# Attention scores spread by an accumulating transfer, with count columns and a filled-in shift, in a graph network kernel

## What is computed

```python
# layer 0: messages of edges, summed by node, then a dense update of every node
messages = mish(mish(cat(x[src], x[dst], edge_attr) @ W1 + b1) @ W2 + b2)
agg = segment_sum(messages, dst)
out = x + mish(cat(x, agg) @ W3 + b3) @ W4 + b4
# layer 1: mean over neighbours, then a normalisation over all nodes by column
agg = segment_sum(x[src], dst) / maximum(deg, 1)
out = agg @ W_l + b_l + x @ W_r
out = (out - mean(out, 0)) * rsqrt(var(out, 0) + EPS) * gamma + beta
out = where(out >= 0, out, 0.01 * out) + x
# layer 2: filters of an edge times rows of its nodes, summed by node (few columns)
# layer 3: attention over the edges, in 8 heads
aw = einsum(q[src], k[dst]); m = segment_max(aw, src)
e = exp(aw - m[src]); out = segment_sum(e / segment_sum(e, src)[src] * v[dst], src)
```

## Time and profile before

| | us |
|---|---|
| runs | 2187.74, 2193.56, 2196.75 |
| median | 2193.56 |
| profiled execution, its own time | 2185.32 |
| its span in the profile | 2183.6 |
| busy: PE, DVE, ACT, POOL | 1809.6, 1495.4, 1149.0, 939.1 |
| share of the span: PE, DVE, ACT, POOL | 83%, 68%, 53%, 43% |
| mean granted TensorE clock | 0.896 |

### The profile page before, as it was taken

The page is one execution under the profiler, slowest core; times in us unless marked ns, Lnnn a source line. Parts: engine busy times, 40 slices in busy tenths (PEclk is TensorE's granted clock), DMA queues, the critical chain, the costliest instruction groups (busy, mean ns, idle before and its releaser), DMA issues. The chain is left out here.

```text
span 2183.6 us, 24152 instructions
## 1 busy us (share of the span) xinstructions
PE 1809.6 (83%) x5525; PEld 939.7 (43%) x5525; DVE 1495.4 (68%) x2634; ACT 1149.0 (53%) x2356; POOL 939.1 (43%) x1051
## 2 busy tenths in 40 slices
PE   5999999599999999999999996932881698888830
PEld 2444444244444444444444443511771354444410
DVE  5365555167777777777777764927985788888857
ACT  1354434255555555555555542224884877777744
POOL 2211101156666666666666665644553022222126
PEclk9999999799999999999999998965555789999965
DMA  7652102534444444444444436664556555554444
GB/s 252 239 194 66 25 11 34 135 131 169 169 169 169 164 161 161 160 164 169 169 169 168 163 137 228 122 112 159 115 108 194 196 179 194 174 184 175 151 146 152
DMA packets 147582, 334.99 MB, mean 153 GB/s; under 512 B 18833, under 2 KB 19314, under 8 KB 146998
## 3 DMA queue, kind: packets, MB, share of 16 engines
q1 hardware_dynamic: 114726, 245.97, 32.4%
q0 software_dynamic: 29440, 83.69, 15.5%
q10 hardware_dynamic: 3344, 4.51, 0.6%
HBM read 181.92 MB, written 152.90 MB: 153 GB/s over the span
## 5 line engine op out<-in xcount | busy, mean ns | idle before, releaser
L668 PE MATMUL d_p_h<-w3a,d_xT 128*128 128x512 f32 x632 | 286.4, 596 | 23.1 <-DMA d_xT<-in_xT 23.1
L668 PE MATMUL d_p_o<-d_w,d_uT 128*128 128x512 f32 x632 | 286.9, 597 | 3.0 <-ACT d_uT L743 3.0
L668 PE MATMUL d_p_p<-d_wr,d_x1T 128*128 128x512 f32 x632 | 285.3, 594 | 0.0
L552 POOL TENSOR_SCALAR d_small<-d_mv 128x1 f32<-128x1 f32 x158 | 80.9, 512 | 301.3 <-DVE d_mv L794 153.3
L825 DVE TENSOR_TENSOR d_zz<-d_yg,d_xbeta 128x512 f32<-128x512 f32 x79 | 136.8, 1732 | 97.4 <-POOL d_yg L876 97.4
L668 PEld LDWEIGHTS d_p_h<-w3a,d_xT 128*128 128x128 f32 x632 | 120.9, 192 | 176.0 <-issue 176.0
L668 PEld LDWEIGHTS d_p_o<-d_w,d_uT 128*128 128x128 f32 x632 | 120.7, 192 | 155.4 <-issue 150.7
L736 ACT ACTIVATE d_yn<-d_y,d_small 128x512 f32<-128x512 f32 x79 | 64.3, 814 | 229.7 <-POOL d_small L557 229.7
L668 PEld LDWEIGHTS d_p_p<-d_wr,d_x1T 128*128 128x128 f32 x632 | 114.5, 191 | 114.5 <-issue 114.5
L764 ACT ACTIVATE d_x<-d_zz,d_small 128x512 f32<-128x512 f32 x79 | 64.3, 814 | 176.6 <-POOL d_small L557 176.6
L284 PE MATMUL m_p_H<-m_xT,m_w 128*128 128x512 f32 x320 | 147.5, 616 | 4.8 <-ACT m_xT L325 4.8
(11 more groups left out here) (285 smaller groups left out, 4231.0 us busy)
## 6 DMA issues: line engine op xcount, KB each, us to landing
state<-d_empty SPq DMA_DIRECT2D x80, 264.0 KB, 2.4
sum<-m_tile_sum SPq DMA_DIRECT2D x10, 2048.0 KB, 7.8
update<-d_empty SPq DMA_DIRECT2D x80, 256.0 KB, 2.3
pair_rows<-p_rows SPq DMA_DIRECT2D x40, 512.0 KB, 3.7
pair_x<-x SPq DMA_DIRECT2D x40, 512.0 KB, 4.6
out_rows<-pair_rows SPq DMA_DIRECT2D x40, 512.0 KB, 2.7
d_xT<-in_xT SPq DMA_DIRECT2D x79, 256.0 KB, 2.8
d_z<-sum SPq DMA_DIRECT2D x79, 256.0 KB, 3.0
```

Of the source, the lines that this page charges most:

```text
L552: nc.gpsimd.tensor_scalar(tmp, var, factor, add, ALU.mult, ALU.add).then_inc(done, 1)
L668: last = nc.tensor.matmul(out[:, :], lhsT[:, c, :], w[:, c, :], start=(c == 0), stop=(c == KB - 1))
```

## The change

The scores are stored as a row of 1024 numbers in DRAM (by a transfer that ACT issues), and one accumulating transfer by GpSimd (`spread_scores`) adds this row to all 128 partitions of `cand`, which ACT has laid out with 0 and `-BIG` (1024 columns now, where `away` had 128). The turn, the 8 matmuls, ACT's copy and DVE's addition go. In the steps of DVE, `pair_means` and `softplus` come ahead of `tile_maximum`; on ACT, `scores_out` comes directly behind `away_from`.

`sum0` gets 16 more columns, `COUNT`, filled with 0 and scatter-added with 1. The dense phase loads them by a transfer of its own for each tile, and DVE multiplies what it adds to the column sums with 1 where the count is 0, else with 0; so the aggregate phase has no old rows to gather and to subtract.

For all pairs but the first three (`PLAIN`) the shift is not added by DVE: at the end of the edge-rows phase DVE makes `quotient = shift / scale`; SP fills the buffer of the pair with it (`pair_fill`, in place of the load), and GpSimd adds `p` with an accumulating transfer (`pair_add_p`).

```diff
+COUNT = 16
...
+PLAIN = 3
...
+    k.sum0 = nc.dram_tensor("sum0_counted", [ROWS, D + COUNT], F32).ap()
...
-                             b3_row.rearrange("p (a d) -> p a d", a=1).to_broadcast([P, some, D])
+                             tile_sum[:, 0:1, :].to_broadcast([P, some, D + COUNT])
...
+                    pool.memset(tile_sum[:, :, D:D + COUNT], 1.0).then_inc(counts_set, 1)
+                    pool.wait_ge(counts_set, 2)
...
-                sp.dma_start(z[b][:, :], rows(k.sum0, i)).then_inc(z_in[b], 16)
+                sp.dma_start(z[b][:, :], rows(k.sum0, i)[:, 0:D]).then_inc(z_in[b], 16)
...
+            def load_count(i, b):
+                if not first(i):
+                    sp.wait_ge(alone_done, i - 1)
+                sp.dma_start(count[b][:, :], rows(k.sum0, i)[:, D:D + COUNT]).then_inc(count_in[b], 16)
...
+                dve.wait_ge(count_in[b], landed(i, b))
+                if not first(i):
+                    dve.wait_ge(acc_done, 2 * i - 2)
+                nc.vector.tensor_scalar(alone[b][:, :], count[b][:, 0:1], 0.0, None, ALU.is_equal).then_inc(alone_done, 1)
+                dve.wait_ge(alone_done, i + 1)
                 dve.wait_ge(row_done, i + 1)
...
-                        nc.vector.tensor_tensor(k.column_acc[0:valid, s, :], k.column_acc[0:valid, s, :],
-                                                part[b][0:valid, :], ALU.add).then_inc(acc_done, 1)
+                        nc.vector.scalar_tensor_tensor(
+                            out=k.column_acc[0:valid, s, :], in0=part[b][0:valid, :], scalar=alone[b][0:valid, 0:1],
+                            in1=k.column_acc[0:valid, s, :], op0=ALU.mult, op1=ALU.add).then_inc(acc_done, 1)
...
-            sp.wait_ge(corrected, 2 * T)
...
-            def gather_old(t):
-                pool.indirect_dma_start(old[:, t, :], None, k.p[:, :], at_rows(k.index[:, 1, t:t + 1])
-                                        ).then_inc(old_in, 16)
-
             pool.iota(dummy_i[:, :], [[0, 1]], base=N + P, channel_multiplier=1).then_inc(dummy_set, 1)
-            for t in range(3):
+            asked = 10
...
-            for t in range(T):
-                gather_old(t)
-                if t % 3 == 2:
-                    gather_x1(asked)
-                    asked += 1
-            pool.wait_ge(old_in, 16 * T)
...
-            dve.wait_ge(old_in, 16 * T)
-            for t in range(T):
-                if t >= 2:
-                    dve.wait_ge(corrected, 2 * t - 2)
-                nc.vector.tensor_tensor(square[t % 2][:, :], old[:, t, :], old[:, t, :], ALU.mult).then_inc(old_sq, 1)
-                correct(0, old[:, t, :], k.minus_share[:, t:t + 1])
-                dve.wait_ge(old_sq, t + 1)
-                correct(1, square[t % 2][:, :], k.minus_share[:, t:t + 1])
...
+def pair_fill(nc, k, sp, j):
+
+    b = j % ROW_BUFS
+    if j >= ROW_BUFS:
+        sp.wait_ge(k.pair_gone[b], 16 * (j // ROW_BUFS))
+    else:
+        sp.wait_ge(k.quotient_done, 1)
+    sp.dma_start(k.pair_rows[b][:, :, :], k.quotient[:, :].rearrange("p (a d) -> p a d", a=1).to_broadcast([P, 2, D])
+                 ).then_inc(k.pair_filled[b], 16)
+
+
+def pair_add_p(nc, k, pool, j):
+    b = j % ROW_BUFS
+    pool.wait_ge(k.pair_filled[b], 16 * filled_times(j))
+    nc.gpsimd.dma_start(k.pair_rows[b][:, :, :], rows_of_pair(k.p, j), accum_op=ALU.add).then_inc(k.pair_added[b], 16)
...
-    dve.wait_ge(k.pair_p_in[b], 16 * (j // ROW_BUFS + 1))
+    if j < PLAIN:
+        dve.wait_ge(k.pair_p_in[b], 16)
+    else:
+        dve.wait_ge(k.pair_added[b], 16 * filled_times(j))
     nc.vector.tensor_tensor(a, a, wide(k.bn_scale), ALU.mult).then_inc(k.pair_scaled, 1)
     dve.wait_ge(k.pair_scaled, j + 1)
-    nc.vector.tensor_tensor(a, a, wide(k.bn_shift), ALU.add).then_inc(k.pair_shifted, 1)
-    dve.wait_ge(k.pair_shifted, j + 1)
+    if j < PLAIN:
+        nc.vector.tensor_tensor(a, a, wide(k.bn_shift), ALU.add).then_inc(k.pair_shifted, 1)
+        dve.wait_ge(k.pair_shifted, j + 1)
     nc.vector.scalar_tensor_tensor(out=a, in0=a, scalar=0.01, in1=a, op0=ALU.mult, op1=ALU.max
...
+            scale, small, n = k.bn_scale[:, :], a[0][:, 0, :], 0
+            for f in (lambda: nc.vector.tensor_tensor(small, scale, scale, ALU.mult),
+                      lambda: nc.vector.tensor_scalar(small, small, 1e-36, 1e-18, ALU.is_lt, ALU.mult),
+                      lambda: nc.vector.tensor_tensor(scale, scale, small, ALU.add),
+                      lambda: nc.vector.reciprocal(small, scale)):
+                f().then_inc(k.quotient_steps, 1)
+                n += 1
+                dve.wait_ge(k.quotient_steps, n)
+            nc.vector.tensor_tensor(k.quotient[:, :], k.bn_shift[:, :], small, ALU.mult).then_inc(k.quotient_done, 1)
...
+            def spread_scores(t):
+                pool.wait_ge(aw_out, 16 * (t + 1))
+                pool.wait_ge(away_done, t + 1)
+                nc.gpsimd.dma_start(cand, k.score_rows[t:t + 1, :].to_broadcast([P, P * HEADS]), accum_op=ALU.add
+                                    ).then_inc(cand_in, 16)
...
+                if 0 <= t + 1 < T:
+                    spread_scores(t + 1)
                 if 0 <= t < T:
                     scatter_state(t)
                     if t + 1 < T:
                         gather_state(t + 1)
                 if step + 2 < T:
                     gather_rows(step + 2)
+                if step + 1 < STEPS:
+                    for j in range(given, given + HERE[step + 1]):
+                        pair_add_p(nc, k, pool, j)
+                    given += HERE[step + 1]
...
-            def turn_scores(t):
-                pe.wait_ge(aw_done, t + 1)
-                nc.tensor.transpose(p_k[0:HEADS, 0:P], k.scores[:, t, :], k.ident[:, :]).then_inc(aw_turned, 1)
-
-            def spread_scores(t):
-
-                pe.wait_ge(aw_out, t + 1)
-                if t:
-                    pe.wait_ge(part_done, t)
-                else:
-                    pe.wait_ge(heads_set, 2)
-                for h in range(HEADS):
-                    last = nc.tensor.matmul(p_S[:, h // 4, (h % 4) * P:(h % 4 + 1) * P], head_rows[0:HEADS, h, :],
-                                            scoresT[:, :], start=True, stop=True)
-                last.then_inc(spread_done, 1)
...
-                act.wait_ge(aw_turned, t + 1)
-                if t:
-                    act.wait_ge(spread_done, t)
-                nc.scalar.activation(scoresT[:, :], p_k[0:HEADS, 0:P], ACT.Copy).then_inc(aw_out, 1)
+                act.wait_ge(aw_done, t + 1)
+                act.dma_start(k.score_rows[t, :].rearrange("(p h) -> p h", h=HEADS), k.scores[:, t, :]
+                              ).then_inc(aw_out, 16)
 
             def away_from(t):
                 if t:
-                    act.wait_ge(cand_done, t)
+                    act.wait_ge(top_done, t)
                 same = k.same_src[:, t, :] if t < T - 1 else k.same_src_last[:, :]
-                nc.scalar.activation(away[:, :], same, ACT.Copy, bias=-BIG, scale=BIG).then_inc(away_done, 1)
+                nc.scalar.activation(cand.rearrange("p (e h) -> p e h", h=HEADS),
+                                     same.rearrange("p (e a) -> p e a", a=1).to_broadcast([P, P, HEADS]),
+                                     ACT.Copy, bias=-BIG, scale=BIG).then_inc(away_done, 1)
...
+                    scores_out(d)
                 if 0 <= c < T:
                     x3_turned_out(c, 0)
                     x3_turned_out(c, 1)
@@ -1847,8 +1877,6 @@
                     tile_normalise(nc, k, act, u)
                 if 0 <= c < T:
                     query_out(c)
-                if 0 <= d < T:
-                    scores_out(d)
...
-                dve.wait_ge(spread_done, t + 1)
-                dve.wait_ge(away_done, t + 1)
-                if t:
-                    dve.wait_ge(top_done, t)
-                nc.vector.tensor_tensor(cand[:, :, :], p_S[:, :, :].rearrange("p a (h e) -> p (a h) e", h=HEADS // 2),
-                                        away[:, :].rearrange("p (a e) -> p a e", a=1).to_broadcast([P, HEADS, P]),
-                                        ALU.add).then_inc(cand_done, 1)
-                dve.wait_ge(cand_done, t + 1)
+                dve.wait_ge(cand_in, 16 * (t + 1))
                 if t >= 2:
                     dve.wait_ge(fall_done, t - 1)
-                nc.vector.tensor_reduce(top, cand[:, :, :], AX_X, ALU.max).then_inc(top_done, 1)
+                nc.vector.tensor_reduce(top, cand.rearrange("p (e h) -> p h e", h=HEADS), AX_X, ALU.max).then_inc(top_done, 1)
...
+                    softplus(a)
                 if 0 <= d < T:
                     tile_maximum(d)
-                if HERE[step]:
-                    pair_means(nc, k, dve, pair)
-                if 0 <= d < T:
                     weigh_values(d)
-                if a < T:
-                    softplus(a)
                 for j in range(pair + 1, pair + HERE[step]):
```

(8 more changed lines are left out.)

77 lines of the change are left out of this document (40 added, 37 removed).

## The result

The changed kernel took 2230.78 us, the median of its runs (2228.61 to 2235.67), beside 2192.33 (2187.74 to 2196.75) for the kernel before. The ratio is 1.0179, with a 95% interval from 1.0150 to 1.0208. The profiled execution took 2228.76 us with a span of 2226.8, which is 43.2 over the 2183.6 before. The medians are only 38.5 apart: the profiled execution of the kernel before took 2185.32, less than any of its other runs.

What follows compares the result with a forecast made beforehand. The values phase was taken as bound by a loop of waits through ACT's list, no engine. 2185.3 - 10.5 + 5 + 12 + 34 = 2225.8, with 8.2 from profiled execution to median 2234 us; range 2184 to 2280.

Steps and rivals of the forecast that it cites:

- Aggregate phase: Twenty gathers and 60 DVE operations go, so the last pair of scatter-adds starts earlier: -10.5 us (-11 to -8).
- Message phase: Six serial scatter-adds at the end with wider rows, 0.8 us more each: +5 us (0 to +12).
- Dense and edge-rows phases: Added count work and the quotient's operations lie under cover: 0 (0 to +3) and 0 (0 to +2) us.
- Start of the values phase: Fill and accumulation behind each other make pairs later in the first four steps: +12 us (0 to +20).
- The steady step: Values phase: 18.85 us a step becomes 20.85, 2.0 more over 17 intervals: +34 us (+5 to +70).
- The clock's term: Values phase: PE idles before the queries, which run partly at half clock, +1.7 us a step (0 to 3.0).
- The floor of 19.15: Values phase step without loss of clock, by DVE's way to `less` and ACT's list: 0.3 us over 18.85.
- The row of scores: Values phase: store 2.2 us, GpSimd's issue and spread 7.0 land at S + 9.3 (S: issue of `scores_out`), 0.6 to spare.
- The full transfer engines (3): Rival, chance 0.13: the transfer engines become the bound in the values phase, a step of 23 us, median 2270.
- The gain (4): Rival, chance 0.15: DVE no longer late, ACT's list sets the values step at 17.1 us, median 2158.
- The rival without a loss of clock (2): Rival, chance 0.20: the same values loop at full clock, 0.3 us more a step, median 2205.
- that all is covered (5): Rival, chance 0.10: values step stays 18.85 us, start slips by 5, the aggregate's gain pays for it, median 2193.

Runs made afterwards that it cites:

- e6: The changed kernel with the spread of the scores taken back, count columns, fills and accumulating loads kept: 2164.28 us.
- e10: e4 with matmuls of 256 columns in TensorE's idle stretches, 4 ahead of the turns and 6 ahead of the queries each step: 2196.75 us.
- e4: The kernel before with the count columns alone, so no old rows in the aggregate phase: 2168.46 us.
- e5: The changed kernel with pairs loaded plain and the shift added by VectorE; spread and count columns kept: 2221.95 us.
- e1: The changed kernel with VectorE's tile_maximum put back ahead of pair_means and softplus: 2231.90 us.
- e3: The changed kernel with matmuls of 256 columns added, 4 ahead of the turns and 6 ahead of the queries each step: 2211.15 us.
- e7: e1 with the store of the scores issued by GpSimd as soon as they are there, not by ScalarE: 2244.84 us.
- e9: e5 with the maximum put first, the edit of e1: 2186.20 us.
- e13: e9 with the matmuls of e3 added, a wait for second_out ahead of them: 2175.93 us.
- e12: e6 with the first 10 pairs loaded plain, not 3: 2154.93 us, ratio 0.983 to the kernel before.
- e2: The changed kernel with cand laid out head by head for a contiguous maximum, the scores stored in 4-byte pieces: 2357.76 us.

## Why the prediction came out as it did

The forecast was 2234 with a range from 2184 to 2280; measured were 2230.78. The sign, the size and the likeliest case held. Not every step behind them did.

- **What bounded the kernel.** Right: the values phase is a loop of waits, no engine's busy time. The fills and accumulations of e6 lie beside the loop and cost nothing in the steady step; ten more matmuls a step do not (e10), so TensorE, 0.87 busy in e4, is close to the loop as well.
- **Aggregate phase.** Right: -11.0 for -10.5, since the last pair now waits for its tile (4.50, for `dst_rows_sb`) and no longer for the pair before it; e4 shows the same 11.3 by itself.
- **Message phase.** Mis-sized: +5 forecast, -1.3 measured, and the last start varies by 4.7 without a change. The serial scatter-adds went from 5.53 to 5.58 apart, where I had 0.8 more each (4.8 to land before, 4.9 now). A row's 64 additional bytes cost by their bytes, at most; the end of the bound that I moved away from was the right one.
- **Dense and edge-rows phases.** Right: +0.1 and +0.7, within what these phases vary by.
- **Start of the values phase.** Right in mechanism: VectorE waits 4.57, 3.93 and 5.68 for its first three accumulated pairs, where the earlier trace rows has 3.46 for a plain one. The fills cost 11.7 up to the fifth `away` beside the spread (e5) and 2.9 without it (e6 against e4), for 12 forecast; up to the first `away` the kernel after loses 4.7.
- **The steady step.** Right in direction, mis-sized, and near the table's row partly by luck. I had +2.0 on 18.85; steps of the same kind went from 18.95 to 21.76, +2.8. Over the first 17 intervals, as many as the sum had, the loss is 47.6 where I had 34. In the total this is made up by the message phase, which I had 6.3 too high, and by the start, if the 12 of the forecast are set beside the 4.7 up to the first `away`. The clock's term held: the queries took 75.0 us in 13 steps, 5.8 each, and 4.1 in the kernel before over 12 steps, so 1.6 for 1.7. But how long TensorE was idle directly ahead of them, from which I argued, does not tell it: they took 5.17 behind 3.00 and 6.53 behind 2.20.
- **The chain behind the step's floor.** The floor of 19.15 was worked out along the wrong chain. I let VectorE run from the merge through the residual without a stop, and put the queries on ScalarE's list only; in truth the residual waits for ScalarE's copy `f_y`, which stands behind the query's copy. So the dip of the clock reaches `less` through VectorE, and the 2.5 us of work that VectorE lost are idle time in its waits for `factor` and `f_y`. The maximum, which I took at 1.22, took 2.00: no row showed a stride of 8, and I had set no bound for it. These 0.8 are as much as lies between +2.0 and +2.8; that they are the cause is not shown, since no run takes the stride away by itself.
- **The row of scores.** I gave it 0.6 us of slack. Its place was right: e1 put the maximum 2.7 us earlier, and the row was late at once by 2.4. Its parts were not: the spread landed 5.3 after its issue, not 7.0, and the store took about 2.1 in one step and 4.7 to 6.5 in the next in most steps, beside the pairs' accumulations, where I had 2.2 for all. By the rule of the Trainium skill ("DMA: Bandwidth & Descriptors", section "Anatomy of one DMA — SWDGE (gpsimd) path") it would be 3.2 for 512 KB; the trace does not agree, with 5.3 here and 6.7 in e5, where the transfer engines were less busy.
- **The rivals.** The full transfer engines (3) did not set the step: e5 took the load from 0.79 to 0.57 and the step got longer. But they were the next cost: e1, e3 and e7 ran into them, and e9 against e1 shows it. The gain (4) was reached by no run with the spread: e9 and e13 have 19.6 and 19.3 a step, where (4) had 17.1, and e13, with order, load and clock all put right, is still 7.5 above e4, which has no spread. The rival without a loss of clock (2) is refuted by the clock of 0.84 and the queries' 5.8, and that all is covered (5) by the longer step.
- **The median against the profiled execution.** I carried 8.2 over from the kernel before. For the changed kernel the distance was 2.0, and for the experiments it lies between -5 and +7: it is the luck of one execution, not a property of the kernel, and should have stood in the range, not in the sum. The errors in the sum (2225.8 forecast, 2228.8 measured for the profiled execution) and in this distance go against each other.

What stays open: how the 0.7 of e13 divide, how much of the +2.8 is the maximum's stride, and in which phase the 6.7 us lie by which e4's median gain exceeds that of its profile.

## What to carry to other kernels

Where waits form a loop, costs lie over each other: a step moved (e1) gained nothing, and a clock restored (e3) gained 0.8 of 2.0 a step, because the next chain stood close behind; only taking them away together (e13) showed what they came to. Replace engine work by a transfer only where the engine is late, and count the transfer's place in its queue: 4 KB behind accumulations of 512 KB landed nearly as late as those did (6.0 and 7.6 in e7). Fill an engine's idle time with work only where there is idle time: ten such matmuls a step gained 20 us in e3 and cost 28 in e10. Of a change with several parts, time each part alone: here one gained 1.0% (e4), a second 0.6% once its start was mended (e12 against e4), and the third, the spread, lost 3.1% (after against e6).

## What the runs showed of the hardware that was not expected

- Fills and accumulating transfers of 512 KB go with a later landing of a small transfer beside them. The median of the 4 KB store on ScalarE's queue was 2.1 beside plain loads of the pairs and 2.4 beside fills and accumulations (e5, after); with the maximum first it was 1.6 and 4.4 (e9, e1). On GpSimd's queue it was 6.0 (e7).
- A store of 1024 pieces of 4 bytes took 12.7 us, one of 128 pieces of 32 bytes 2.4.
- VectorE's maximum over 1024 columns took 1.22 us for columns behind each other (e2) and 2.00 for columns 8 apart.
- In the first steps with the spread, matmuls added to TensorE kept the granted clock at 1.00 (e13), where e9 had 0.83; in e4 they raised it from 0.84 to 0.96 there and gained no time (e10).
- A scatter-add of 128 rows of 2112 bytes landed in 4.9 us, of 2048 bytes in 4.8.
